# A fused graph-attention, linear-attention and expert kernel: two orders exchanged in every edge step, and three orders at the ends of phases

## The reference

```
xn = layernorm(x)
x  = x + gnn(xn, edge attributes) + mix(xn)
x  = x + ffn(layernorm(x))

gnn:  fs = xn @ W_n, in 8 heads of 32;  el, er = fs . attn_l, fs . attn_r  (4 values a head)
      e  = leaky(sum_t (el[src] + er[dst] + em) * mask / 3)
      a  = exp(e - segment_max(e)[dst]) / segment_sum(...)[dst]
      out = segment_sum(fs[src] * a)
mix:  linear attention: softmax of q over a head's features, softmax of k over the nodes,
      context = k^T v, out = q context Wout, layernorm
ffn:  8 experts, each relu(bn(x W1)), relu(bn(. W2)), . Wo, weighted by a softmax of x Wr
```

## Time and profile before

| | |
|---|---|
| median of three runs | 3161.24 us |
| the profiled execution | 3170.54 us, of which 3168.9 us are the span |
| PE busy, DVE busy, POOL busy, ACT busy | 2874.6, 2638.7, 1852.1, 1700.9 us |
| phases | nodes to 366.67 us, edges to 2257 us, experts to the end |
| steps of the edge phase | first scan of step 1 at 406.65 us, of step 124 at 2223.24 us |
| gathers in the edge phase | 1408, the first at 368.51 us, the last at 2203.55 us |
| stored groups (`store_ahead`) | 26 of 1152 KB, median 4.8 us from issue to landing |
| granted PE clock, mean | 0.971 |

### The profile page before, as it was taken

The page is one execution under the profiler, slowest core; times in us unless marked ns, Lnnn a source line. Parts: engine busy times, 40 slices in busy tenths (PEclk is TensorE's granted clock), DMA queues, the critical chain, the costliest instruction groups (busy, mean ns, idle before and its releaser), DMA issues. The chain is left out here.

```text
span 3168.9 us, 76579 instructions
## 1 busy us (share of the span) xinstructions
PE 2874.6 (91%) x21350; PEld 2376.5 (75%) x21351; DVE 2638.7 (83%) x4799; ACT 1700.9 (54%) x5754; POOL 1852.1 (58%) x3341
## 2 busy tenths in 40 slices
PE   8996589998999999999899999898599999999999
PEld 5565377776777777777777777776388888888899
DVE  5676698998999998899999999898587777777776
ACT  5552256665666665666666666665543333333343
POOL 3888688888888888888888888887000000000000
PEclk9998899999999999999999999999799999999999
DMA  8678867676776767676667676665211000000000
GB/s 312 211 252 298 307 193 202 202 208 197 206 212 199 208 195 197 199 206 199 203 196 205 199 207 206 199 203 156 76 52 34 21 22 21 22 21 18 18 23 10
DMA packets 275943, 500.38 MB, mean 158 GB/s; under 512 B 80679, under 2 KB 177474, under 8 KB 269008
## 3 DMA queue, kind: packets, MB, share of 16 engines
q0 software_dynamic: 85456, 282.69, 30.8%
q1 hardware_dynamic: 190336, 215.88, 21.4%
HBM read 410.81 MB, written 87.57 MB: 157 GB/s over the span
## 5 line engine op out<-in xcount | busy, mean ns | idle before, releaser
L972 POOL DMA_INDIRECT gat<-scratch_table,idx x1360 | 1323.6, 973 | 239.0 <-issue 229.9
L1325 PE MATMUL ps_s<-msg,oh 128*128 128x272 f32 x4000 | 1029.0, 406 | 106.0 <-ACT tmp L1038 55.9
L1325 PEld LDWEIGHTS ps_s<-msg,oh 128*128 128x128 f32 x4000 | 742.7, 193 | 255.5 <-ACT tmp L1038 107.6
L1047 ACT ACTIVATE acc<-acc,sc 128x33 f32<-128x33 f32 x2000 | 458.8, 340 | 224.2 <-DVE acc L1161 222.3
L1610 ACT ACTIVATE h<-ps_h,fsh,fsc 128x512 f32<-128x512 f32 (+1 forms) x416 | 291.1, 751 | 508.8 <-PE ps_h L1824 508.8
L1173 DVE TENSOR_TENSOR msg<-gat,ps_m 128x2048 f32<-128x2048 f32 x250 | 559.3, 2277 | 0.0
L1563 POOL DMA_DIRECT2D out<-y x13 | 9.9, 759 | 897.2 <-DVE y L1778 897.2
L1038 ACT ACTIVATE tmp<-ps_s,sc 128x33 f32<-128x33 f32 x2000 | 386.7, 305 | 17.2
L1027 ACT CAST oh<-ps_o 128x1024 f32<-128x1024 bf16 x250 | 259.3, 1037 | 139.2 <-PE ps_o L1264 137.7
L1653 DVE CAST h_hi<-h 128x1024 fp32r<-128x1024 f32 (+1 forms) x208 | 137.2, 660 | 201.9 <-ACT h L1610 201.8
L1186 DVE TENSOR_TENSOR_SCAN runm<-penr,ps_e 16x1024 f32<-16x1024 bf16 x125 | 284.3, 2274 | 12.8
(11 more groups left out here) (224 smaller groups left out, 5319.8 us busy)
## 6 DMA issues: line engine op xcount, KB each, us to landing
d16r<-scratch_dst SPq DMA_DIRECT2D x250, 256.0 KB
scratch_acc<-acc SPq DMA_DIRECT2D x250, 136.0 KB
scratch_ahead<-stage SPq DMA_DIRECT2D x26, 1152.0 KB, 4.8
gat<-scratch_ahead POOLq DMA_DIRECT2D x26, 1152.0 KB
edge<-in_edge SPq DMA_DIRECT2D x250, 88.0 KB
gat<-scratch_table,idx POOLq DMA_INDIRECT x1360
scratch_table<-stage POOLq DMA_DIRECT2D x49, 144.0 KB, 5.3
xq<-in_xT SPq DMA_DIRECT2D x7, 896.0 KB, 11.4
```

The source lines that it names most:

```text
L972: pool.indirect_dma_start(out=gat[:, s, c, :], out_offset=None, in_=scr["table_rows"], in_offset=bass.IndirectOffsetOnAxis(ap=rows[:, at:a ...
L1047: act.mul(acc[:, new, cols], acc[:, old, cols], sc[:, j, 0, h:h + 1]).then_inc(scaled, 1)
L1325: last = pe.matmul(ps_s[j][:, 0:SUMS], oh[:, s, j, c, :], msg[:, 2 * (s % 2) + j, c, :], start=(c == 0), stop=(c == C - 1), skip_group_che ...
```

## The change

Five edits.

1. In a PE step `turn_maxima(k)` stands before `source_terms` of k+1.
2. In a DVE step `differences(k)` stands before `logits(k+1)`.
3. `EARLY` is 17 instead of 18: the last of the seven turns of SP holds a `reload` alone, each later `store_ahead` moves up by one place, and number 25 comes after all stores of mixed rows.
4. `load_first_sums` is cut in two: `xm` is loaded at the head of SP's step 121, `am` at the head of its step 125 (before: both at the head of step 124).
5. In block 0 of the experts the parts of `prepare` for block 1 come later, by the table `OPENING`: none at x = 0 and 1, part 0 at x = 2, parts 1 and 2 at x = 3, part 3 at 4, part 4 at 5, part 5 at 6, parts 6 and 7 at 7.

```
-EARLY = 18
+EARLY = 17
...
             for c in range(NT // XC):
-                store_ahead(FIRST_BESIDE + c)
+                if FIRST_BESIDE + c < EARLY:
+                    store_ahead(FIRST_BESIDE + c)
                 reload(c)
...
+            def load_mixed():
+
+                sp.dma_start(opening.xm[:, :, :], scr["xmix"][0:B].rearrange("a p c -> p a c")).then_inc(opening_in, 16)
+
             def load_first_sums():
 
-                sp.dma_start(opening.xm[:, :, :], scr["xmix"][0:B].rearrange("a p c -> p a c")).then_inc(opening_in, 16)
                 sp.dma_start(opening.am[:, :, :], scr["acc"][0:B].rearrange("a p c -> p a c")).then_inc(opening_in, 16)
...
-                if isinstance(k, int) and k == K - 1:
+                if isinstance(k, int) and k == K - SLOTS:
+                    load_mixed()
+                if isinstance(k, int) and k == K:
                     load_first_sums()
...
-                if more:
-                    logits(k + 1, (s + 1) % SLOTS)
                 if alive:
                     differences(k, s)
                 if more:
+                    logits(k + 1, (s + 1) % SLOTS)
                     over_terms(k + 1)
...
+                if alive:
+                    turn_maxima(k, s)
                 if more:
                     source_terms(at, groups)
-                if alive:
-                    turn_maxima(k, s)
                 if summing:
                     segment_sums(k - 1, s0, 1, range(BEFORE, C))
...
+        OPENING = [(), (), (0,), (1, 2), (3,), (4,), (5,), (6, 7)]
...
-                    if following:
+                    if opening:
+                        for part in OPENING[x]:
+                            prepare(1, 1, B, part)
+                    elif following:
                         prepare(b + 1, 1 - s, following, x)
```

## The result

The changed kernel takes 3224.4 us (median; 3222.5 to 3230.7) against 3161.8: ratio 1.020, 95% interval 1.019 to 1.022, 62.7 us slower. The forecast was 3202.8 with 3168 to 3224. The direction came out as said, and so did the mechanism in the edge step. The size is 21 us short, and the time lies 0.4 us beyond the upper end.

The account below looks back on a forecast made before the run. Two close bounds were seen in the edge phase, gathers' supply at 14.77 us a step and consumers at 14.12, and PE in the experts' phase. 37.0 + 0 - 1.9 + 6.5 = +41.6 gave a 3202.8 us median, range 3168 to 3224.

Parts of the forecast that it names:

- Two bounds, slack of 0.65 us: Edge steps: gathers' supply at 14.77 us, consumers at 14.12; a consumer up to 0.65 slower costs nothing, beyond that each step pays.
- Edits 1 and 2, +37.0 us: Edge step: 0.95 us longer, 15.07, above the supply's 14.77, so waits for POOL vanish and step 124 starts 37.0 us later.
- two pauses in each step: VectorE in the edge step: waits of 0.26 us before differences (for ps_m) and 0.57 before logits (for ps_z).
- The dependent start, +0.12: VectorE in the edge step: over_terms need logits' result, so start 0.04 us behind their end, not 0.08 before it: 0.12.
- The start of the phase, forecast 0: From the node phase's end to the first scan of step 1: no term in the sum, so no change.
- Edit 3, -1.9: Node phase: store_er follows at about 356.7 and the phase ends 1.9 us earlier, near 364.8.
- the two cases that the prediction gave: Node phase's end: -5.1 us if store_er lands as before, -0.3 if it queues behind the 1152 KB of number 25.
- Edit 4, 0: Loads of xm and am: moving them hides nothing, 0; 3 to 4 us back if the supply were still the bound.
- Edit 5, +6.5: Block 0 of the experts: later parts of prepare cost 6.5 us in sum, bounds +1 and +10.
- -5.1, +9.1 and +2.5: PE's waits in block 0: 5.1 us less for wT, 9.1 more before part 2, 2.5 more at x = 7.
- the 15.20: Upper bound of a usual edge step in us, if segment_sums also push absn: +53 us over the steps.

Follow-up runs that it names:

- pad_small: The kernel before with two memsets that compute nothing on VectorE ahead of messages, order unchanged: 3162.4 against 3160.7 us, 1.000.
- edge_orders_2: The kernel before with both new orders of the edge step (PE's and VectorE's) and nothing else: 3215.4 against 3159.8 us, 1.017.
- best_3: The changed kernel with the edge step's two orders put back and another OPENING table for block 0 of the experts: 3153.5 against 3160.9 us, 0.998.
- dve_alone_4: The kernel before with VectorE's order alone changed, differences ahead of the next logits: 3149.0 against 3160.9 us, 0.996.
- combo: The kernel of best_3 with VectorE's order of dve_alone_4 added: 3142.1 against 3160.7 us, 0.995.

## Why the prediction fell short

The step that failed is a term of the sum, not the path: source_terms were put at 1.03 us in their new place and take 1.13. That is 12 us of the 18.6 by which the two profiles differ from the +41.6 of the sum (60.2 us); the rest is +4 more in the edge step, +1.8 at the phase's start, +0.3 at its end, +1.0 in block 0 and -0.9 in the node phase. The medians differ by 62.7, 2.5 more, because the profile of before lies 9 us above its median and that of after 6.

- *Two bounds, slack of 0.65 us.* Right as far as VectorE's own time goes (pad_small: +0.4 us a step, 1.000). That the slack ends at 0.65 was not measured. The 14.77 is a mean that takes in the last step, 24.94 us with the wait of 8.44 for the last gathers. What failed is that the supply is independent of the consumer's order: with differences ahead, the 1360 gathers take 1753.7 us instead of 1770.8. In the changed kernel this had no part, since its steps are above both.
- *Edits 1 and 2, +37.0 us.* Mechanism right: two pauses in each step, no wait for POOLq, waits of POOL instead. The pause ahead of differences was put at 0.26, and the start after join moved from 0.08 ahead of its end to 0.18 behind it: 0.26. The term that was mis-sized is source_terms, taken as 1.03 from a step in which a product of segment_sums ran ahead of them. Behind turn_maxima they take 1.13, in 124 of 125 steps. The forecast had the row: it cites four products that took 1.13 behind a wait, and used them for the clock alone. That is 0.10 x 123 = 12 us. The other 4 are a longer reduction (0.69 against 0.67, 1.6 us) and five steps of 16.0 to 16.1 us in which turn_maxima came 0.8 to 1.2 late.
- *The dependent start, +0.12.* over_terms start 0.03 us behind logits' end, as forecast from 0.04, where unrelated operations overlap by 0.08. These rows are what speaks against no cost for such a wait: over 117 steps the median is 0.034 behind, against 0.08 ahead. With no cost and source_terms at 1.13 the step would be 15.05, and it took 15.20.
- *The start of the phase, forecast 0.* +1.8 us, of which 1.4 in step 0, where the orders cost more than in a usual step (14.83 against 13.41 us from the first scan to the second step's; 14.83 in edge_orders_2 too). I had counted steps from step 1 on. pad_small, with no order changed, has 14.75 there too, so the orders are not needed for it; why is open.
- *Edit 3, -1.9.* Measured -2.8, but that end scatters by as much with the order unchanged. VectorE's wait of 14.63 us fell to 8.09. store_er was issued at 356.63, as forecast, and the phase ended 7.21 us later instead of 4.91: between the two cases that the prediction gave.
- *Edit 4, 0.* 0, since no step waits for the last gathers. Where one does it gave back 1.5 to 1.9, not 3 to 4 (best_3).
- *Edit 5, +6.5.* Measured +7.5. The terms were -5.1, +9.1 and +2.5; the rows show 7.30 less 2.20 = -5.1, +8.98 and +2.42. The remaining 1.2 is mostly half clock behind the new wait (the eight products of L1805 took 1.94 us at a granted clock of 0.50, 1.04 before), which I had counted as only moved.
- *Range.* The upper end is the plain sum of the upper bounds: 53 - 0.3 + 10 = +62.7 on 3161.2 is 3224, though the prediction calls it "less their joint extremes". The edge step alone took its whole bound, by a cause that the bound was not made for: the 15.20 stood for segment_sums that push absn. So small things decided the last 0.4 us, among them the +1.8 that had no place in the sum. That the measured +62.7 equals the sum of the bounds is chance.

## What to carry over

A duration belongs to what ran ahead of it: when an instruction moves behind other neighbours, take its duration from a row with those neighbours. Test the two halves of a pair of reorderings apart: here one half costs 0.27 us a step more than both (in unhindered steps), and the other is a gain. And where two engines bound a kernel closely, don't hold one's pace fixed while changing the other's order.

## What the runs showed of the hardware

- The order of VectorE's operations changed the pace at which POOL issues gathers by 1% (1770.8 to 1753.7 us for 1360), with the same instructions. Long issues number 210, 198 and 202 in before, pad_small and best_3, and 145, 148 and 162 in dve_alone_4, combo and edge_orders_2, all three with differences ahead of logits. POOL's instructions overlap one-hots as often (359 times in before, 353 in dve_alone_4), but fewer of these overlaps are long (186 and 125). Why this order shifts where they meet is open.
- The 123 steps took 1798.8 us in dve_alone_4 and 1797.1 in combo. On the same two chips best_3 and pad_small, with VectorE's old order, took 1816.2 and 1815.2. The total of dve_alone_4 is 12 us below that of before, less than these 17 us: step 0 gives up 1.6 of them (15.05 against 13.41), and the rest is not accounted for.
- The four products of source_terms take 1.13 us behind short products or a wait (123 steps of edge_orders_2) and 1.03 behind a long one (114 steps of dve_alone_4). Behind the long one their first weight load starts 0.23 us ahead of the first product.
- On chips with slow transfers the order of VectorE that gains 12 us here costs 0.3%, and the one that costs 56 us here costs 18. Why transfers were slow there is open.
